# A gated cross-attention kernel on one core: small dependent steps of Vector and GpSimd become single instructions with semaphores of their own, and all four hand-written orders ahead of the main loop change

## What is computed

```python
# layer 0, attention: context attends to itself, and mixes the normalised x
q, k = ctx @ Wq.T + bq, ctx @ Wk.T + bk
x = x + t_attn * (softmax(q @ k.T) applied to layernorm(x))
# layer 0, feed-forward: ternary weights, activations rounded to 8 bits
def bit_linear(x, w):                     # w is scaled by mean|w| and rounded to -1, 0, 1
    xn = rms(x); s = 127 / max|xn|
    return round(xn * s) / s @ wq.T
gate, up = split(bit_linear(layernorm(x), gate_w))
x = x + t_ffn * bit_linear(silu(gate) * up, down_w)
# layer 1, attention: 16 heads of 128, q and k normalised by rms
x = x + t_attn * (softmax(rms(xn @ Wq) @ rms(ctx @ Wk).T / sqrt(128)) @ (ctx @ Wv) @ Wo)
# layer 1, feed-forward: 64 experts, the best 8 of each token, and one shared expert
x = x + t_ffn * (sum_e w_e * expert_e(xn) + shared(xn))
```

## Time and profile before

| what | value |
|---|---|
| median of 3 runs | 620.29 us (620.06 to 620.79) |
| the profiled execution's own time | 620.25 us |
| its span, first to last instruction | 618.5 us |
| TensorE matmul busy | 605.6 us, 98% |
| VectorE busy | 482.0 us, 78% |
| ScalarE busy | 422.2 us, 68% |
| GpSimd busy | 233.8 us, 38% |
| granted TensorE clock | 1.00 of full speed |

### The profile page before, as it was taken

One profiled execution on the slowest core, in us unless ns is written; L12 is line 12 of the kernel. 1 busy time (PEld: TensorE's weight loads), 2 busy tenths in 40 slices (PEclk: granted clock), 3 DMA queues, 4 the chain that ended last, 5 costly groups with the idle time before them and its releaser, 6 DMA issues.

```text
span 618.5 us, 11618 instructions
## 1 busy us (share of the span) xinstructions
PE 605.6 (98%) x3644; PEld 524.2 (85%) x3644; DVE 482.0 (78%) x1139; ACT 422.2 (68%) x1080; POOL 233.8 (38%) x280
## 2 busy tenths in 40 slices
PE   8889999999999999999999999999999999999997
PEld 6657899999999999999998888888887888887886
DVE  4999889888777687788775787778877677777776
ACT  6998998988888888889898444364444444443442
POOL 5899798666666666556662020000000000000000
PEclk9999999999999999999999999999999999999999
DMA  8503221000000000000030445443756466554630
GB/s 294 198 26 103 78 77 37 17 1 2 2 2 2 2 2 2 1 2 1 6 125 2 140 159 147 150 149 100 214 166 171 113 171 166 165 154 148 199 128 34
DMA packets 33653, 56.47 MB, mean 91 GB/s; under 512 B 12800, under 2 KB 13504, under 8 KB 33600
## 3 DMA queue, kind: packets, MB, share of 16 engines
q1 hardware_dynamic: 33312, 55.82, 29.6%
q10 hardware_dynamic: 288, 0.00, 0.0%
HBM read 53.45 MB, written 1.31 MB: 89 GB/s over the span
## 4 chain that ended last, share of the span: by engine, by line
PE 87%; DVE 6%; issue 2%; POOL 2%; ACT 2%; DMA 1%; SPq 0%; DVEq 0%; ACTq 0%; POOLq 0%
PE bank L296 24%; PE bank L298 24%; PE bank L297 24%; PE bank L897 4%; PE bank L872 2%; PE bank L864 2%; PE bank L938 1%; PE bank L824 1%; ACT att L1489 1%; DVE hs L1974 1%; PE bank L817 1%; DMA wqk<-in_qk 1%; PE bank L797 1%; PE bank L744 1%; PE bank L777 1%
## 5 line engine op out<-in xcount | busy, mean ns | idle before, releaser
L1537 ACT ACTIVATE inter_hi<-inter 128x512 fp32r<-128x512 f32 x63 | 39.8, 632 | 140.6 <-DVE inter L2165 140.6
L296 PE MATMUL bank<-xnT_hi,front_hi 128*128 128x512 f32 (+1 forms) x260 | 102.0, 392 | 0.0
L298 PE MATMUL bank<-xnT_hi,front_lo 128*128 128x512 f32 (+1 forms) x260 | 101.7, 391 | 0.0
L297 PE MATMUL bank<-xnT_lo,front_hi 128*128 128x512 f32 (+1 forms) x260 | 101.7, 391 | 0.0
L2169 DVE TENSOR_TENSOR inter_lo<-inter,inter_hi 128x512 fp32r<-128x512 f32 x63 | 43.6, 692 | 37.5 <-ACT inter_hi L1537 37.0
L1489 ACT ACTIVATE att<-bank,shift,rq 128x256 f32<-128x256 f32 x128 | 71.3, 572 | 1.9 <-DVE shift L2055 1.9
L557 POOL TENSOR_TENSOR att<-att,rowinv 128x512 f32<-128x512 f32 x60 | 62.9, 1064 | 12.1 <-DVE rowinv L2065 12.1
L2138 DVE TENSOR_TENSOR prod<-gate_s,bank 128x512 f32<-128x512 f32 x63 | 43.2, 686 | 22.0 <-PE bank L298 20.0
L2048 DVE TENSOR_REDUCE rowmax<-bank 128x2 f32<-128x512 f32 x64 | 43.5, 684 | 20.7 <-PE bank L298 20.3
L297 PEld LDWEIGHTS bank<-xnT_lo,front_hi 128*128 128x128 f32 x260 | 48.9, 188 | 11.3
L298 PEld LDWEIGHTS bank<-xnT_hi,front_lo 128*128 128x128 f32 x260 | 48.8, 188 | 11.3
(11 more groups left out here) (270 smaller groups left out, 1816.5 us busy)
## 6 DMA issues: line engine op xcount, KB each, us to landing
w_all<-w_rows SPq DMA_DIRECT2D x128, 128.0 KB, 2.9
raw<-in_expert_w SPq DMA_DIRECT2D x32, 384.0 KB, 3.5
wvo_raw<-in_expert_w SPq DMA_DIRECT2D x16, 384.0 KB, 3.6
e_more<-in_expert_w SPq DMA_DIRECT2D x16, 384.0 KB, 3.6
raw<-in_head_qk SPq DMA_DIRECT2D x8, 384.0 KB, 3.4
wvo_raw<-in_head_vo SPq DMA_DIRECT2D x4, 384.0 KB, 3.0
w_keep<-in_head_vo SPq DMA_DIRECT2D x4, 384.0 KB, 3.3
gate_raw<-in_gate_wT SPq DMA_DIRECT2D x2, 704.0 KB, 9.0
```

The lines of the kernel that those rows point to most:

```text
L296: pe.matmul(out, l_hi, r_hi_, start=start, stop=False, skip_group_check=True)
L297: pe.matmul(out, l_hi, r_lo_, start=False, stop=False, skip_group_check=True)
L298: return pe.matmul(out, l_lo, r_hi_, start=False, stop=stop, skip_group_check=True)
L1537: act.activation(inter_hi[:, slot, :], inter[:, slot, :], ACT.Copy).then_inc(a_Ihi, 1)
```

## The change

Every function of VectorE or GpSimd that held two or more dependent steps is cut so that each step is a call of its own. The wait between the steps stays, but it is on a semaphore of its own, and the second step can stand later in the list, behind other work. New calls are `aggr_0`, `aggr_1`, `aggr_2`, `inv_A`, `inv_max_1`, `inv_max_2`, `inv_scale` on VectorE and `power_0` to `power_3`, `limit_1`, `limit_2`, `times_rk` on GpSimd; `times_g1`, `normalise_0` and `normalise_1` now take one tile instead of two. The instructions themselves and their number stay the same, but for the matmuls of `keep_busy`: there were 14 in four places, and there are 7 in one. The four lists of the front are written anew. The loop and the experts change only in the names of semaphores. Some banks of PSUM are assigned differently in the front.

The diff, cut to its core:

```diff
+            def token_stats(i0, i1, done):
+                for i in range(i0, i1):
+                    ins = dve.bn_stats(stats[:, i, :], x[:, i, :])
+                ins.then_inc(done, 1)
+            def token_mean(i0, i1):
+                for i in range(i0, i1):
+                    ins = dve.bn_aggr(mv[:, i, :], stats[:, i, :])
+                return ins
...
             def stats_0(b):
                 dve.wait_ge(l_x[b // 2], 16)
-                tile_stats(2 * b, 2 * b + 2).then_inc(v_pw1, 1)
+                token_stats(2 * b, 2 * b + 2, v_st0)
+            def aggr_0(b):
+                dve.wait_ge(v_st0, b + 1)
+                token_mean(2 * b, 2 * b + 2).then_inc(v_pw1, 1)
...
+            def inv_A(b):
+                dve.wait_ge(a_eA, 2 * b + 2)
+                dve.reciprocal(invA[:, b, :], sumA[:, b, :]).then_inc(v_nA, 1)
             def norm_A(b):
-                dve.wait_ge(a_eA, 2 * b + 2)
-                link(dve, dve.reciprocal(invA[:, b, :], sumA[:, b, :]))
+                dve.wait_ge(v_nA, 2 * b + 1)
...
             def absmax_1(b):
                 c = slice(2 * b, 2 * b + 2)
-                link(dve, dve.tensor_reduce(T[:, 3, c], w1[:, c, :], AX.X, ALU.max, apply_absolute_value=True))
-                link(dve, dve.reciprocal(T[:, 10, c], T[:, 3, c]))
+                dve.wait_ge(v_tg, 2 * b + 2)
+                dve.tensor_reduce(T[:, 3, c], w1[:, c, :], AX.X, ALU.max, apply_absolute_value=True).then_inc(v_am, 1)
+            def inv_max_1(b):
+                c = slice(2 * b, 2 * b + 2)
+                dve.wait_ge(v_am, 2 * b + 1)
+                dve.reciprocal(T[:, 10, c], T[:, 3, c]).then_inc(v_am, 1)
...
             def root_0(b):
                 pool.tensor_scalar(negm[:, c], mv[:, c, 0], -1.0, 0.0, ALU.mult, ALU.add)
-                link_g(pool, pool.tensor_scalar(vare[:, c], mv[:, c, 1], 1.0, EPS, ALU.mult, ALU.add))
+                pool.tensor_scalar(vare[:, c], mv[:, c, 1], 1.0, EPS, ALU.mult, ALU.add).then_inc(g_va0, 1)
+            def power_0(b):
+                c = slice(2 * b, 2 * b + 2)
+                pool.wait_ge(g_va0, b + 1)
                 pool.tensor_tensor(rstd[:, c], vare[:, c], minus_half[:, 0:2], ALU.pow).then_inc(g_pw1, 1)
```

The list of VectorE from its start, and around the first tiles of the second product:

```diff
             stats_0(0)
             stats_0(1)
-            max_A(0, 6)
-            max_A(1, 1)
-            max_A(2, 3)
+            aggr_0(0)
+            max_A(0, 3)
+            max_A(1, 2)
+            aggr_0(1)
+            max_A(2, 6)
+            inv_A(0)
             norm_A(0)
             stats_0(2)
+            inv_A(1)
+            aggr_0(2)
+            stats_0(3)
...
+            absmax_1(0)
+            stats_1(1)
+            inv_max_1(0)
+            weight_scale(1, 0, INTER * HID)
             scales_1(0)
+            aggr_1(1)
             round_1(0)
...
+            inv_max_1(3)
             absmax_2(2)
-            absmax_1(3)
+            absmax_2(3)
             scales_1(3)
+            inv_max_2(1)
             round_1(6)
+            times_up_0(5)
+            add_down(0, 5)
+            stats_2(0)
+            add_down(1, 0)
+            scales_2(1)
             round_1(7)
```

GpSimd's list around `limit_1(3)`, which `silu_0(6)` waits for (`scale_back_1(3)` held both of its steps before):

```diff
             times_gain(3)
-            root_2(1)
+            times_rk(0)
+            power_2(1)
+            limit_2(0)
+            times_gain(4)
             scale_back_1(3)
-            times_gain(4)
+            scale_back_2(1)
             root_2(2)
+            limit_1(3)
             root_3(0)
+            power_3(0)
             normalise_1(0)
+            normalise_1(1)
```

More of the change, by code:

```diff
@@ L610, in _ @@
             rms_k(1)
+            times_rk(1)
+            root_2(3)
+            power_2(3)
+            rms_k(2)
+            times_rk(2)
             scale_back_2(2)
-            root_2(3)
+            rms_q(0)
+            limit_2(2)
             scale_back_2(3)
-            rms_k(2)
-            rms_q(0)
             pool.wait_ge(t_q2, 8)
@@ new lines, in _ @@
+            query_key(1, 0, 4)
+            query_key(0, 1, 0)
+            query_key(1, 1, 5)
+            energy(0, 3)
+            energy(1, 2)
+            energy(2, 6)
+            pe.wait_ge(a_eA, 2)
+            energy(3, 3)
+            turn_rows_0(0, 4)
+            turn_att(0, 7)
+            mix(0, 4)
+            turn_att(1, 6)
+            turn_rows_0(1, 7)
+            sum_abs([0, 1], 2)
+            pe.wait_ge(v_abs, 1)
+            mix(1, 2)
+            turn_att(2, 5)
+            sum_abs([2], 0)
@@ L1020, in _ @@
             up_0(0)
-            pe.wait_ge(v_wsi, 2)
-            turn_att(3, 5)
+            mix(2, 4)
             gate_0(1)
-            pe.wait_ge(a_s1, 2)
-            turn_q1(2, 0)
             up_0(1)
-            proj_k(0, 4, True)
+            fuse_vo(0, 6)
+            turn_rows_0(3, 7)
+            pe.wait_ge(v_h1, 2)
+            turn_q1(2, 2)
+            pe.wait_ge(a_x0, 4)
+            turn_q1(3, 7)
             gate_0(2)
-            turn_rows_0(3, 5)
-            turn_q1(3, 6)
+            turn_att(3, 4)
@@ L2191, in _ @@
-            max_A(3, 4)
-            add_A(0, 0)
-            weight_scale(0, 7, 2 * INTER * HID)
+            weight_scale(0, 2, 2 * INTER * HID)
+            inv_scale(0)
             stats_1(0)
-            norm_A(3)
+            inv_A(3)
+            aggr_1(0)
             times_g1(0)
-            add_A(1, 0)
+            times_g1(1)
+            add_A(1, 2)
             absmax_1(0)
+            stats_1(1)
+            inv_max_1(0)
+            weight_scale(1, 0, INTER * HID)
             scales_1(0)
+            aggr_1(1)
@@ L2200, in _ @@
             round_1(0)
-            stats_1(1)
             round_1(1)
-            times_g1(1)
+            times_g1(2)
+            times_g1(3)
             low_w(0)
             absmax_1(1)
+            norm_A(3)
+            inv_max_1(1)
+            inv_scale(1)
             scales_1(1)
-            weight_scale(1, 5, INTER * HID)
+            round_down()
             round_1(2)
-            round_down()
             times_up_0(0)
-            low_w(1)
-            add_A(2, 6)
-            times_up_0(1)
@@ L2214, in _ @@
-            low_m(0, 7)
-            stats_1(2)
-            round_1(3)
-            times_g1(2)
+            add_A(2, 4)
+            stats_1(2)
+            times_up_0(1)
+            aggr_1(2)
+            round_1(3)
+            times_g1(4)
+            times_g1(5)
+            low_w(1)
             absmax_1(2)
+            inv_max_1(2)
+            low_m(0, 6)
+            scales_1(2)
             times_up_0(2)
-            scales_1(2)
+            round_1(4)
+            round_1(5)
             absmax_2(0)
-            add_A(3, 7)
@@ L2236, in _ @@
             scales_1(3)
+            inv_max_2(1)
             round_1(6)
-            round_1(7)
-            times_up_0(5)
-            add_down(0, 1)
-            absmax_2(3)
-            add_down(1, 4)
-            stats_2(0)
+            times_up_0(5)
[3 more added lines that the diff above has]
+            scales_2(1)
+            round_1(7)
             stats_2(1)
-            scales_2(1)
             round_2(2)
-            low_w(2)
-            times_up_0(6)
@@ L2249, in _ @@
-            key_gain()
-            absmax_2(4)
-            low_m(1, 6)
-            round_2(3)
-            first_mean_k(1)
+            aggr_2(0)
+            aggr_2(1)
+            low_m(1, 7)
+            key_gain()
+            round_2(3)
+            absmax_2(4)
+            first_mean_k(1)
+            times_up_0(6)
+            low_w(2)
             times_up_0(7)
             low_rows(0, 0, 4)
-            low_k(0, 5)
             absmax_2(5)
+            add_down(2, 7)
+            low_k(0, 6)
```

752 lines of the change are left out of this document (401 added, 351 removed).

## The result

The kernel after takes 616.25 us (median of 4 runs, 616.19 to 618.08) against 620.46 us before (4 runs, 620.06 to 620.79): ratio 0.994, 95% interval 0.9929 to 0.9952. The same kernel was run again beside the first experiments, under the label after_again: 616.85 us (6 runs, 616.07 to 617.15) against 620.31 us, ratio 0.9935, interval 0.992 to 0.9951. The forecast was 617.1 us, with a range of 614.8 to 619.4.

The account below looks back on a forecast made before the run. VectorE, with ScalarE near, was taken to set the first 60 us. The terms 4.6 - 0.8 - 0.4 - 0.5 + 0.3 = 3.2 us gave 620.3 - 3.2 = 617.1 us, range 614.8 to 619.4.

Parts of the forecast that it names:

- Step one: On VectorE, a wait for the instruction directly in front costs 0.11 us, or 0.10 us for tiny steps.
- no effect: Rival: VectorE's waits hide nothing that counts, or TensorE's new order loses the gain again; 620.3 us, chance 0.12.
- Steps two and three: VectorE up to `low_rows(0)`: 42 waits in the old list, 4.6 us; seven stay in the new one, 0.8 us.
- Step four: VectorE's waits for others: 0.4 us more at `weight_scale(0)`, 0.5 more at `absmax_2(3)`, 0.3 won back from `square_h`.
- The meetings: VectorE steps lengthened beside GpSimd products fall anew with each order; 0.88 us either way, left out of the sum.
- slower: Rival: GpSimd becomes the bound at `times_gain(3)`, deciding from a wait of 4.9 us on; 622.9 us, chance 0.08.
- Step five: ScalarE can finish `copy_rows(0)` 2.2 us earlier; seven fewer `keep_busy` cost nothing; GpSimd's splits bring some 0.03 us each.
- Step six: Loads on SyncE queued behind the later `fuse_vo(0)` cost nothing, since their reader `split_w(2)` moves back further.
- Step seven: Behind 60.31 us TensorE can win at most 0.99 us of idle time and lose about as much; taken as 0.
- ScalarE takes over: Rival: ScalarE keeps half of its idle time, so `low_rows(0)` comes at most 2.5 us earlier; 617.8 us, chance 0.17.
- more than that: Rival: VectorE keeps half of the exposed waits, loses nothing to new ones, TensorE gains; 5.3 us, 615.0 us, chance 0.15.

Follow-up runs that it names:

- joined_vector: Kernel after with VectorE's split steps joined again, restoring the 42 waits; the new order and GpSimd's single steps stay: 619.73 us, ratio 0.9986.
- more_waits: Kernel before with 42 added waits of VectorE on its own last instruction up to `low_rows(0)`: 626.4 us, ratio 1.0093.
- split_old_order: Kernel before with VectorE's steps split and moved behind one or two neighbours; old order on all engines, GpSimd's steps joined: 624.07 us, ratio 1.0054.
- joined_gpsimd: Kernel after with GpSimd's powers, limits and key gains joined into the functions of before: 624.17 us, ratio 1.0054.
- no_filler: Kernel after without the seven `keep_busy` matmuls that it kept: 618.05 us, ratio 0.9954.
- more_waits_filled: Kernel of more_waits with five filler products ahead of `turn_q1(4)` on TensorE, behind the idle stretch they were meant to fill: 626.43 us, ratio 1.0107.

## Why the prediction was right, step by step

**Where the time goes.** The view was right: the front sets the start of TensorE's dense part, and VectorE sets the front. Of the 3.6 us of span, 3.03 lie ahead of the first product.

**Step one, the price.** 0.11 us for a wait on the instruction directly in front, from pairs in the earlier trace rows, holds: 42 more of them made VectorE's stretch 4.5 us longer, meetings taken off, 0.11 each; the 33 of joined_vector give the same. The rule that the prediction weighed against it (the Trainium skill, "VectorE: DVE Perf Modes", section "The DRAIN you can't avoid") would have made more_waits 0 us slower; it was 6.1. The rival *no effect* falls with it.

**Steps two and three, how many.** Both counts hold: the traces have about 42 of the short gaps before and 7 after. In VectorE's own list they do take what was said: 3.8 us for the 33 of joined_vector. Putting them back moved `low_rows(0)` by only 2.8 us and the median by 2.9, because a part of them then covers waits for other engines. So as what the waits are worth to the kernel, the term was 0.9 to 1.0 us too high.

**Step four, what appears and goes.** Expected was -0.4 - 0.5 + 0.3 = -0.6 us. VectorE's waits for others, without the short gaps, grew by 0.8 us (from 1.4 to 2.2), so the size is right. The wait of `absmax_2(3)`, put between 0 and 1.3 us and taken as 0.5, is 0.93. The idle time ahead of `weight_scale(0)`, where I had put 0.4 us more, is gone; in its place there are 0.6 us ahead of `add_A(0)`, its neighbour. The 0.62 us ahead of `times_up_0(4)` are gone in full, not by half. One thing had no term: VectorE began 0.46 us later than before. In the first profile of the same kernel it began at 7.98 us, so this is a matter of the execution.

**The meetings.** The prediction left them out of the sum and gave them 0.88 us of either sign. The three kinds of step listed above take 2.0 us less after than before, and `low_w` (three of them) 1.2 us more (1337 against 951 ns), so that the net is 0.8 us in favour, of the size given. But joined_vector has the same meetings to within 0.1 us (353, 574, 159 and 1324 ns) and reaches `low_rows(0)` only 0.2 us before the old kernel, so the new order gives most of that back. What I had not seen is how large they can get: they took 2.6 us more in split_old_order than in the kernel before, and with 3.1 us more of waits for others they turned a gain into a loss. The prediction's *slower* rival named a wait for GpSimd at `times_gain(3)` as the way to it. joined_gpsimd is that case, with a wait of 2.68 us, and it already decides there, not at 4.9: my price took only VectorE's idle time at this step and left out the later waits, the meetings, TensorE's stop and its clock behind it.

**Step five, whether the others follow.** ScalarE is down to 0.77 us of idle time (under 1 was said). TensorE's fillers: I said the seven that went cost nothing. The clock of the kernel after is 1.00 where they stood, which fits, but no run puts them back. The seven that stayed were priced at 0.4 us each at most and not asked for what they do: they keep the clock up from 22 to 26 us, and without them the kernel is about 1 us slower, by the clock or by the meetings that move with it (no_filler). GpSimd's splits were called little, some 0.03 us each. As a price of a wait that may be so, but as an order it was wrong: joining them delays `times_gain(3)` by 2.7 us and costs 7.3 us in the median (624.17 against 616.85), more than all that the change gains. This is the step that a reader should mistrust in such a prediction.

**Step six, moved work with transfers.** Costed at nothing, and that holds: behind the loads of the start TensorE, ScalarE, VectorE and GpSimd wait for no transfer up to 160 us.

**Step seven, the rest.** I took 0 for all that follows the first product; it was 0.57 us, 0.46 of it less idle time of TensorE in the 95.69 us behind it.

So the mechanism was right, and the number came out that near by luck as well. By the trials, a term that was 1.0 us too high (the waits, 2.8 instead of 3.8) met two that were too low: the rest of the change up to `low_rows(0)` (+0.2 in joined_vector instead of -0.6) and the rest of the front (0.6 instead of 0). This split takes the effects as if they added up, which no run tests. Of the rivals, *ScalarE takes over* fell with its idle time, and *more than that* asked for 5.3 us, where the span gave 3.6 and the medians 3.5 and 4.2.

## What to carry to other kernels

Where an engine's list is dense, a wait on the instruction directly in front costs about 0.1 us, and one unrelated step between the two hides it; count them before looking for arithmetic to save, and expect the kernel to get back less than their sum, here 2.9 of 3.8 us. Splitting steps is worth it only together with the order of the engines that exchange work with this one: VectorE's single steps in the old order, and the new order with GpSimd's steps joined, were each slower than the kernel before. Before moving a VectorE step to fill a wait for GpSimd, look what GpSimd runs at the new place, since the wait can come back as a longer step. How much of the gain the new lists of TensorE and ScalarE carry by themselves was not tried.

## What the runs showed of the hardware

**Meetings of VectorE and GpSimd.** Some VectorE steps on operands in SBUF wait out a GpSimd product beside which they start. They then end a fixed time after it: 0.02 us (`scales_1`, 128x2), 0.15 (`round_1`, 128x256), 0.38 (`round_2`, 128x704) and 0.81 (`low_w`, 128x768), the same to 0.01 us in every trace here in which at least 0.25 us of the product was left. So 0.35 us become 1.74, 1.69 and 1.10, 0.18 become 0.99 and 0.87, and 0.95 become 2.12: a step of two columns waits as long as a large one. Reductions (0.87 us), `bn_stats` (0.41), reciprocals (0.17) and steps that read PSUM (0.94) were not stretched by the same products. It goes the other way too: GpSimd's power of two columns took 1.29 to 1.69 us instead of 0.70 beside a `low_w`, and its limit 1.59 instead of 0.30. The Trainium skill, "SBUF — State Buffer", section "Who interferes with whom", calls the port pair that the two engines share an exclusive lock; the traces agree.

**The clock after an idle stretch.** TensorE's granted clock was 0.50 to 0.53 behind idle stretches of 2.08, 2.13 (no_filler and more_waits_filled), 2.29 and 3.17 us, and 1.00 behind one of 1.40 us. In between the length does not decide: behind stretches of 1.86 to 1.89 us it was 1.00 in two profiles and 0.50 in split_old_order, and behind one of 2.12 us in more_waits it was 1.00. Filling the stretch won about 1 us in joined_gpsimd, meetings included, and the fall cost nothing that shows in more_waits, where VectorE was later.
